# Spread bf16 operands for the destination one-hots, x in five loads, and the gate products of x ahead of the adjacency loop

## The reference

```
agg = segment_sum(x[src], dst)                     # layer 0: sum over 20,000 edges
gates = x4 @ gate_w                                # layer 1: 512 x 8 gate matrix
agg = segment_sum(x[col] * vals[:, None], row)     # layer 2: the same edges, weighted
```

## Time and profile before

| | |
|---|---|
| median of 3 runs | 2312.99 us (2309.54 to 2313.89) |
| profiled execution, its own time | 2310.99 us |
| its span, first to last instruction | 2309.0 us |
| PE busy over the span | 2171.3 us (94%) |
| DVE busy over the span | 1606.3 us (70%) |
| edge block, until the last DVE instruction | 0 to 38.97 us |
| adjacency block | 38.97 to about 196 us |

### The profile page before, as it was taken

One profiled execution on the slowest core, in us unless ns is written; L12 is line 12 of the kernel. 1 busy time (PEld: TensorE's weight loads), 2 busy tenths in 40 slices (PEclk: granted clock), 3 DMA queues, 4 the chain that ended last, 5 costly groups with the idle time before them and its releaser, 6 DMA issues.

```text
span 2309.0 us, 32827 instructions
## 1 busy us (share of the span) xinstructions
PE 2171.3 (94%) x11871; PEld 1906.3 (83%) x11871; DVE 1606.3 (70%) x2619; ACT 1059.3 (46%) x1862; POOL 634.5 (27%) x1081
## 2 busy tenths in 40 slices
PE   3997998597979999999999999999999999999998
PEld 3887996467858888888888888888888888888887
DVE  7996355736487776777777667777776777777665
ACT  0335334344354544545554444554544455554443
POOL 0554000011133233223322322243233223323320
PEclk9999999598989999999999999999999999999999
DMA  2000201151001111111111111111111111111111
GB/s 71 3 2 1 73 1 64 65 173 45 28 23 37 46 51 37 37 49 48 37 38 59 38 37 37 60 37 37 46 51 37 38 58 39 37 39 58 37 37 54
DMA packets 70701, 102.00 MB, mean 44 GB/s; under 512 B 5519, under 2 KB 40927, under 8 KB 70543
## 3 DMA queue, kind: packets, MB, share of 16 engines
q1 hardware_dynamic: 67243, 94.20, 12.8%
q0 software_dynamic: 3040, 5.19, 0.7%
q10 hardware_dynamic: 260, 0.51, 0.1%
HBM read 92.14 MB, written 7.74 MB: 43 GB/s over the span
## 4 chain that ended last, share of the span: by engine, by line
PE 72%; DVE 1%; ACT 1%; issue 0%; DVEq 0%; ACTq 0%
PE psum L528 24%; PE psum L529 24%; PE psum L530 24%; DVE x_forms L2224 0%; DVE x_parts L2224 0%; ACT w_forms_hi L1845 0%; PE psum L1972 0%; DVE x_forms_lo L2235 0%; ACT x_forms_hi_late L1834 0%; DVE node_z L2219 0%; ACT f_rows L522 0%; DVE x_rows L2244 0%; DVE stats L486 0%; ACT L1922 0%; DVE x_forms L2228 0%
## 5 line engine op out<-in xcount | busy, mean ns | idle before, releaser
L530 PE MATMUL psum<-w_hi,hidden_lo 128*125 128x512 f32 x1280 | 505.2, 395 | 0.0
L529 PE MATMUL psum<-w_lo,hidden_hi 128*125 128x512 f32 x1280 | 504.8, 394 | 0.0
L528 PE MATMUL psum<-w_hi,hidden_hi 128*125 128x512 f32 x1280 | 504.6, 394 | 0.0
L529 PE MATMUL psum<-x_forms_lo,w_forms_hi 128*128 128x418 f32 x1280 | 453.6, 354 | 0.0
L1782 POOL TENSOR_TENSOR w_forms<-w_raw 128x128 f32<-128x128 f32 x192 | 107.0, 585 | 1159.1 <-PE psum L530 597.7
L2212 DVE SCALAR_TENSOR_TENSOR x_rows<-psum,leaf_by_token,x_rows 125x512 f32<-125x512 f32 x320 | 233.8, 747 | 258.3 <-PE psum L530 258.3
L1895 ACT ACTIVATE hidden<-psum 128x418 f32<-128x418 f32 (+1 forms) x320 | 164.5, 514 | 487.9 <-PE psum L530 485.3
L530 PEld LDWEIGHTS psum<-w_hi,hidden_lo 128*125 128x125 f32 x1280 | 237.1, 185 | 60.0
L528 PEld LDWEIGHTS psum<-w_hi,hidden_hi 128*125 128x125 f32 x1280 | 237.1, 185 | 56.6 <-issue 0.5
L529 PEld LDWEIGHTS psum<-w_lo,hidden_hi 128*125 128x125 f32 x1280 | 237.3, 185 | 55.1
L2185 DVE TENSOR_TENSOR hidden_lo<-hidden,hidden_hi 128x418 fp32r<-128x418 f32 (+1 forms) x384 | 256.5, 693 | 21.8 <-ACT hidden_hi L1917 21.8
(11 more groups left out here) (346 smaller groups left out, 3511.5 us busy)
## 6 DMA issues: line engine op xcount, KB each, us to landing
w_raw<-in_w SPq DMA_DIRECT2D x128, 512.0 KB, 3.9
expert_raw<-in_experts SPq DMA_DIRECT2D x8, 1024.0 KB, 5.6
expert_results_d<-expert_results SPq DMA_DIRECT2D x16, 160.0 KB, 4.8
x_rows<-in_x SPq DMA_DIRECT2D x1, 2500.0 KB
c_rows_d<-c_rows SPq DMA_DIRECT2D x10, 250.0 KB
W_raw<-in_gnn_W SPq DMA_DIRECT2D x4, 512.0 KB, 4.1
W_raw<-in_gnn_W SPq DMA_DIRECT2D x1, 2048.0 KB, 9.5
b_by_token<-in_b SPq DMA_DIRECT2D x8, 256.0 KB, 3.9
```

The source lines that it names most:

```text
L528: t.matmul(out, stat[0], mov[0], start=start, stop=False, skip_group_check=again)
L529: t.matmul(out, stat[0], mov[1], start=False, stop=False, skip_group_check=again)
L530: return t.matmul(out, stat[1], mov[0], start=False, stop=stop, skip_group_check=again)
```

## The change

The three loads of the edge lists, the constants and x are issued in another order: SP issues four loads that the chain waits for, then x as five loads of two tiles each, with `i10f` behind the first of them. The thirteen small loads move to ACT's queue. The cast of `i10f` moves from the head of the DVE chain to behind `lohi`, with a semaphore of its own.

The four big DVE instructions get other operands. POOL spreads `rem` over 32 columns as bf16 (`rem_by_column`), ACT spreads the first two weight parts (`parts_by_column`), and DVE compares and multiplies these bf16 arrays; the product with the third part stays as it was. All tile work on x (transposes, copies, gate products, the copy of the results) leaves the adjacency loop and stands at the end of the edge block, with three buffers for `x_T` and three PSUM banks.

```diff
-            v.wait_ge(loaded, 16 * len(loads))
-            s.mark(v.tensor_copy(g.i10[:, :], i10f[0:EB, :]))
...
+            v.wait_ge(loaded, 16 * len(loads))
+            s.mark(v.tensor_copy(iota16[:, :], g.iota32[0:EB, :]))
...
+            v.wait_ge(i10_loaded, 16)
+            s.mark(v.tensor_copy(g.i10[:, :], i10f[0:EB, :]))
+            d = g.D_all[:, 0:NB, :, :]
+            v.wait_ge(rem_spread, 1)
+            s.then(v.tensor_tensor(d[:, :, 0, :], rem16[:, :, :],
+                                   iota16[:, :].unsqueeze(1).to_broadcast(shape), ALU.is_equal))
+            for c in range(2):
+                v.wait_ge(part_spread, c + 1)
+                s.mark(v.tensor_tensor(d[:, :, 1 + c, :], d[:, :, 0, :], part16[:, c, :, :], ALU.mult))
+            s.mark(v.tensor_tensor(d[:, :, 3, :], d[:, :, 0, :], parts[:, :, 2:3].to_broadcast(shape), ALU.mult))
...
+            v.wait_ge(x_gated, NT)
+            v.tensor_copy(g.x_gates[:, :], g.psum[0:TR, 7, 0:(NT + 1) * NE])
+
+        @block.gpsimd
+        def _(q):
+            q.wait_ge(g.steps.semaphore, at.rem)
+            q.tensor_copy(rem16[:, :, :], rem[:, :].unsqueeze(2).to_broadcast(shape)).then_inc(rem_spread, 1)
+
+        @block.scalar
+        def _(a):
+            def spread_part(c, made):
+                a.wait_ge(g.steps.semaphore, made)
+                a.activation(part16[:, c, :, :], parts[:, :, c:c + 1].to_broadcast(shape),
+                             ACT.Copy).then_inc(part_spread, 1)
+
+            def copy_x(i):
+                a.wait_ge(x_turned, i + 1)
+                if i >= 3:
+                    a.wait_ge(x_gated, i - 2)
...
+            for to, of in later_loads:
+                a.dma_start(to, of).then_inc(later_loaded, 16)
+            spread_part(0, at.part0)
+            copy_x(0)
+            copy_x(1)
+            spread_part(1, at.part1)
+            for i in range(2, NT):
+                copy_x(i)
...
+            for k in range(KD):
+                t.matmul(g.psum[0:TR, 7, NT * NE:(NT + 1) * NE], g.ones[:, 0:TR], g.gate[:, k, :],
+                         start=k == 0, stop=k == KD - 1)
+            turn_x(0)
+            turn_x(1)
+            for i in range(NT):
+                if i + 2 < NT:
+                    turn_x(i + 2)
+                gate_x(i)
...
-                if j == 0:
-                    if i == 0:
-                        t.wait_ge(g.x_loaded, 16)
...
-                if j == 2:
-                    t.wait_ge(x_copied, i + 1)
```

More of the change, by code:

```diff
@@ L224, in phase_edges, with x_bank @@
     ]
[L226 to L230, removed]
+    shape = [EB, NB, WIN]
+    def x_bank(i):
+        return 4 + i % 3
     with nc.Block() as block:
@@ L236, in _ @@
                 sp.dma_start(to, of).then_inc(loaded, 16)
-            for to, of in later_loads:
-                sp.dma_start(to, of).then_inc(later_loaded, 16)
-            sp.dma_start(g.x_rows[:, :, :], g.x.rearrange("(t p) d -> p t d", p=TR)).then_inc(g.x_loaded, 16)
+            for i in range(0, NT, 2):
+                sp.dma_start(g.x_rows[:, i:i + 2, :], g.x[i * TR:(i + 2) * TR, :].rearrange("(t p) d -> p t d", p=TR)).then_inc(
+                    g.x_loaded[i // 2], 16)
+                if i == 0:
+                    sp.dma_start(i10f[:, :], g.consts_d[:, C_I10:C_Q]).then_inc(i10_loaded, 16)
         @block.vector
@@ L264, in _ @@
             s.mark(v.tensor_copy(halves(g.key[:, 0:NB]), table[:, 0]))
-            s.mark(v.tensor_copy(halves(rem[:, :]), table[:, 1]))
+            at.rem = s.mark(v.tensor_copy(halves(rem[:, :]), table[:, 1]))
             s.then(v.tensor_copy(halves(wcol[:, :]), table[:, 2]))
-            s.then(v.tensor_copy(parts[:, :, 0], wcol[:, :]))
+            at.part0 = s.then(v.tensor_copy(parts[:, :, 0], wcol[:, :]))
             s.then(v.tensor_tensor(wres[:, :], wcol[:, :], parts[:, :, 0], ALU.subtract))
-            s.then(v.tensor_copy(parts[:, :, 1], wres[:, :]))
+            at.part1 = s.then(v.tensor_copy(parts[:, :, 1], wres[:, :]))
             s.then(v.tensor_tensor(wres2[:, :], wres[:, :], parts[:, :, 1], ALU.subtract))
@@ L322, in _, with turn_x, gate_x @@
             t.transpose(g.psum[:, 3, 128:256], g.b1rows[:, :], g.ident[:, :]).then_inc(turned, 1)
+            def turn_x(i):
+                t.wait_ge(g.x_loaded[i // 2], 16)
+                if i >= 3:
+                    t.wait_ge(x_copied, i - 2)
+                for k in range(KD):
+                    ins = t.transpose(g.psum[:, x_bank(i), k * TR:(k + 1) * TR], g.x_rows[:, i, k * 128:(k + 1) * 128],
+                                      g.ident[0:TR, 0:TR])
+                ins.then_inc(x_turned, 1)
+            def gate_x(i):
+                t.wait_ge(x_copied, i + 1)
+                for k in range(KD):
+                    ins = t.matmul(g.psum[0:TR, 7, i * NE:(i + 1) * NE], xT[:, i % 3, k, :], g.gate[:, k, :],
+                                   start=k == 0, stop=k == KD - 1)
+                ins.then_inc(x_gated, 1)
+            for k in range(KD):
+                t.matmul(g.psum[0:TR, 7, NT * NE:(NT + 1) * NE], g.ones[:, 0:TR], g.gate[:, k, :],
+                         start=k == 0, stop=k == KD - 1)
+            turn_x(0)
[4 more added lines that the diff above has]
+                gate_x(i)
 def phase_adjacency(nc, sem, g):
@@ L365, in _ @@
             v.reg_mov(n, 1)
[L366 removed]
+            for x_in in g.x_loaded:
+                v.wait_ge(x_in, 16)
             bounds = group_bounds(v, regs[0], 0)
@@ L2372, in gnn_ffn_kernel @@
         g.psum = ctx.enter_context(nc.psum_tensor("psum", [128, 8, 512], F32))
-        g.x_loaded, g.W2_loaded = sem("x_loaded"), sem("W2_loaded")
+        g.x_loaded, g.W2_loaded = [sem(f"x_loaded{i}") for i in range(NT // 2)], sem("W2_loaded")
         g.steps = Steps(sem("vector_steps"))
```

42 lines of the change are left out of this document (13 added, 29 removed).

## The result

The changed kernel takes **2317.24 us** (median of 9 runs, 2315.22 to 2320.54), the kernel before 2312.44 (9 runs, 2309.20 to 2313.89). The ratio of the two is 1.0026 (1.0018 to 1.0034), so 4 to 8 us slower; the medians are 4.8 apart. The forecast was 2315.3, slower by 2.3. The profiled execution of the changed kernel took 2318.03 us, its span 2316.2.

What follows compares the result with a forecast made beforehand. DVE's chain bounds the edge block and mostly the loop; after the change PE's x path ends the block. Block end +6.6, loop start -1.8, loop -2.5 give +2.3 on 2312.99: 2315.3 us, range 2306 to 2321.

Steps and rivals of the forecast that it cites:

- the saving is not cashed: Edge block, DVE's four big instructions: bf16 saves up to 8 us, but the x path on PE ends later.
- the start gives back: Loop start: PE finds its first one-hot pair 1.1 us behind DVE's start instead of 2.9, so -1.8 us.
- Rivals 2 and 3: Rival 3: edge block, POOL spreads `rem` at its two-input rate, 11.2 us not 5.1; +6.1, 2321.4 us; chance 0.12.
- rival 2: Edge block: POOL's one-input copy doesn't hold DVE up, x path ends 4.5 us earlier; 2310.8 us; chance 0.15.
- Rival 1: Edge block's x stretch: PE rises to its fast level, the block ends at 38.8; total -6.7, 2306.3 us; chance 0.14.
- the loop, -2.5: Adjacency loop: without nine x tiles on PE, DVE's waits for it shrink; between 0 and 3.2 us, taken as -2.5.
- 6.6: Edge block's end: PE's x path ends it at 45.6 and not 38.97, 6.6 us later.
- 17.9: Edge block, DVE chain: `lohi` done at 17.9, the chain winning 3.3 us by loads and losing 4.5 to POOL's hold.
- the first subtraction: Edge block: POOL's spread holds DVE's first two-input instruction, the weight cut's subtraction, until about 14.65; costs 4.5 us.

Runs made afterwards that it cites:

- the third experiment: The changed kernel with one-hots built from the old f32 and broadcast operands, no spreads; new loads and x move stay: 2314.28 us, 1.0008 of the kernel before.
- The fifth experiment: The changed kernel with 100 zero matmuls on PE while it waits for `lohi` and ten more per x tile: 2311.37 us, one execution.
- The fourth experiment: The changed kernel with one POOL addition per loop window instead of two, leaving out the third weight part: 2299.30 us, one execution.
- the second and third experiments: The second: the changed kernel with POOL's spread of `rem` waiting for `lohi`, not `rem`: 2314.48 us, 1.001 of the kernel before.

## Why the prediction was right and wrong

**What was right.** The direction, the place and the bound. x on PE ends the block, 9.08 us behind DVE's last own work (forecast 9), and the block ends at 45.40 (forecast 45.6). DVE finds its comparison and first products at 2.81 us for 5.47, and the saving is not cashed: with the old operands and x moved, DVE is still early (the third experiment). The second spread ends at 27.30 (forecast 27.4). The first loop matmul is 1.28 behind DVE's first one-hot (forecast 1.1), so the start gives back 1.66 (forecast 1.8). Rivals 2 and 3 are out: POOL's cast does hold DVE, and takes 4.45. The sign that was named for rival 2, L280 at 0.33 us, did show all the same, because the hold fell on the instruction before. Rival 1 stayed a rival: PE kept its slow pace through 26 us of x work in which it hardly stopped. The fifth experiment shows the other pace with 100 large matmuls ahead and ten more in each tile, and that it is worth 5.7 us at the block's end.

**The step that failed: the loop, -2.5.** From first to last window the changed loop takes 146.76 us against 146.53, so the term is +0.2: -0.25 from the second window on, and +0.48 in the first, where the ten matmuls behind the first 40 still took 1.22 us and not 0.72, which is PE's pace again. The step read: "DVE's waits for it are 4.2 ... at most 3.2 us, at least 0 if DVE only meets POOL instead". Upper end and lower end were right and the choice between them wrong. The waits did go (3.7 to 0.6 us from the second window on, 3.1 of the 3.2), but DVE then ran into POOL's additions, and its instructions grew by as much. The step had also counted only the waits for the pairs: DVE waited for PE another 5.6 us in four places with the extra one-hot (L379), and these hardly changed (5.3). The reason given for the choice, that the waits stand behind the windows with x work, tells where they arise, not what stands behind them. A row of the kernel before pointed at it: the mean of L379, 898 ns, where this instruction takes 0.55 us in the first window, with POOL still idle:

```profile
42.44 0.55 DVE L379 TENSOR_SCALAR src_onehot_more<-i,key 125x1280 bf16<-125x1280 f16 x1
```

The fourth experiment shows that POOL is what sets this pace; the table shows that x doesn't.

With +0.2 for -2.5 the sum is 6.6 - 1.8 + 0.2 = 5.0, where 5.19 was measured at the end of the loop and 4.8 between the medians.

**Smaller misses that cancelled.** The chain started at 6.50, not 5.9: the fourth load took 4.2 us from issue to landing, not 3.5. POOL took 4.45, not 5.1. Together `lohi` ended at 18.17, not 17.9, so that 17.9 was met by luck in part. What POOL held up was not the first subtraction (two inputs in SBUF) but already the cast before it, which has one; the subtraction took its 0.33. The Trainium skill (SBUF — State Buffer, Who interferes with whom) lets casts of one input in a two-port mode contend too, and whoever issues first holds the shared ports for the whole instruction. The 4.41 us agree; whether the cast ran in such a mode no row shows. A tile of x took 2.41 and not 2.47, the loads of x came in time, and the wait for a small load on ACT's queue, which the prediction didn't price, stayed hidden, by the late `lohi` alone (the second and third experiments).

**What the prediction did not see** is that the change had a gain in it. Its rivals varied prices within the change as a whole; none of them separated the spreads from the x move. The spreads and the reordered loads, with x left in the loop, are 6.5 us faster than before, and with ACT in POOL's place 8.5. The move of x spoils this by ending the block later than DVE does; it also puts ACT's copies ahead of the second spread, for which DVE waits 2.84 us, but that is hidden behind the first.

## What to carry to other kernels

Work that rode in a loop for nearly nothing cost its full price, at the slow pace, when it was moved to where an engine works alone: compare the loop's length with and without it, not the waits it seems to cause. Before a wait is booked as a gain, ask what the waiting engine meets next; a mean far above the length of the same instruction alone points at it. Here a large spread cost the same on ACT as on POOL, and only the one on POOL held up DVE's chain of small steps.

## What was not expected of the hardware

- A one-input DVE cast of 160 elements, f32 to bf16, was held for 4.41 us by a one-input cast on POOL. In the other order POOL waited: its cast took 4.98 us and not 4.45 beside a DVE cast of 0.81 us that had started 0.14 before.
- PE was busy without a gap from 28 to 44 us of the changed kernel with transposes and products of eight columns, and each tile took 2.41 us to the end; with 100 matmuls of 128 columns ahead and ten in each tile, it took 1.87. The clock column reads 1.00 in both stretches (28 to 44 us here, 24 to 38 there), so the durations are what tells the two paces apart.
- PE came to the loop at the slow pace in every kernel. Behind a stop of 3.08 and 3.37 us the first 40 matmuls took 3.96 and 4.33 us, where they take 2.40 from the second window on, although PE had been at the fast pace right before the stop.
